# A graph attention layer with a routed feed-forward: where normed input, bias and beta are added for the tiles ahead of the blocks, and the step of the first block

## What is computed

```python
# _layernorm(x): (x - mean) / sqrt(var + 1e-5);  msgs: attention sums of each node, 4 heads of 64
out = msgs.reshape(N, H * D) @ Wo + bo
h = out + _layernorm(x)
gnn = (h - mu) / jnp.sqrt(var + 1e-05) * gamma + beta
x1 = x + gnn
xt = _layernorm(x1)
logits = xt @ Wr + br                      # 8 experts, the top two, weights from a softmax
# the expert network norms once more, then for each of its two experts e:
y_e = gelu(xe @ W1[e] + b1[e]) @ W2[e] + b2[e]      # 256 -> 1024 -> 256
result = x1 + sum(weight_e * y_e)
```

## Time and profile before

| | us |
|---|---|
| median of 3 runs | 3803.58 |
| the runs | 3799.91 to 3803.76 |
| the profiled execution | 3804.72 |
| its span, first to last instruction | 3802.4 |

### The profile page before, as it was taken

One profiled execution on the slowest core, in us unless ns is written; L12 is line 12 of the kernel. 1 busy time (PEld: TensorE's weight loads), 2 busy tenths in 40 slices (PEclk: granted clock), 3 DMA queues, 4 the chain that ended last, 5 costly groups with the idle time before them and its releaser, 6 DMA issues. The chain is left out here.

```text
span 3802.4 us, 76627 instructions
## 1 busy us (share of the span) xinstructions
PE 3098.0 (81%) x21156; PEld 2146.9 (56%) x21156; DVE 1690.1 (44%) x6041; ACT 1507.6 (40%) x4739; POOL 1962.7 (52%) x2036
## 2 busy tenths in 40 slices
PE   8777787778777777877777777787667998899898
PEld 6444444444444444444444444444347898888798
DVE  6154444444444444444444444444475554553222
ACT  5333333333333333333333333333336565564232
POOL 6345555555555555655555555555345444432222
PEclk9888888888888888888888888888758999999999
DMA  6556766676666666666667666666475666665664
GB/s 221 164 150 187 191 190 184 186 191 189 185 185 191 189 185 188 187 192 185 189 187 190 188 185 187 190 188 185 138 230 151 203 203 184 194 180 156 194 181 131
DMA packets 292073, 700.68 MB, mean 184 GB/s; under 512 B 44040, under 2 KB 139679, under 8 KB 291796
## 3 DMA queue, kind: packets, MB, share of 16 engines
q0 software_dynamic: 151888, 455.79, 43.4%
q1 hardware_dynamic: 140036, 243.15, 21.0%
HBM read 632.80 MB, written 65.96 MB: 184 GB/s over the span
## 5 line engine op out<-in xcount | busy, mean ns | idle before, releaser
L246 POOL DMA_INDIRECT e_kv<-d_kv,e_idx x1566 | 1496.1, 955 | 1132.3 <-PE psA L496 668.5
L496 PE MATMUL psA<-e_kv,e_probT 128*32 128x128 f32 x6264 | 529.2, 286 | 297.9 <-issue 292.3
L393 DVE TENSOR_REDUCE e_small<-psD 128x1 f32<-128x384 f32 x261 | 145.5, 558 | 1219.6 <-remote 1208.6
L461 PE MATMUL psK<-consts,e_kv 128*128 128x128 f32 x3132 | 606.6, 327 | 3.3 <-ACT QT L266 1.0
L302 ACT ACTIVATE e_carried<-psA,e_small 128x130 f32<-128x130 f32 x261 | 96.7, 370 | 1135.1 <-PE psA L496 1115.4
L496 PEld LDWEIGHTS psA<-e_kv,e_probT 128*32 128x32 f32 x6264 | 199.9, 108 | 532.8 <-issue 503.8
L461 PEld LDWEIGHTS psK<-consts,e_kv 128*128 128x128 f32 x3132 | 427.5, 166 | 116.4 <-issue 110.0
L1975 PE MATMUL f_psY<-f_w,f_hT 128*128 x1680 | 396.6, 390 | 38.2 <-ACT f_hT L1570 22.1
L1500 POOL DMA_INDIRECT out<-f_y,f_whose x105 | 166.8, 1589 | 479.0 <-DMA out<-f_y,f_whose 281.7
L1962 PE MATMUL f_psH<-f_xT,f_w 128*128 128x128 f32 x3360 | 404.3, 280 | 0.4 <-issue 0.4
L1570 ACT ACTIVATE f_hT<-f_psH,f_b 128x128 f32<-128x128 f32 x840 | 237.6, 372 | 411.0 <-PE f_psH L1962 333.1
(11 more groups left out here) (281 smaller groups left out, 4330.2 us busy)
## 6 DMA issues: line engine op xcount, KB each, us to landing
f_w<-in_W SPq DMA_DIRECT2D x113, 1024.0 KB
e_rows<-d_feat SPq DMA_DIRECT2D x174, 288.0 KB
e_kv<-d_kv,e_idx POOLq DMA_INDIRECT x1566
d_accs<-e_accs SPq DMA_DIRECT2D x87, 195.0 KB
f_xs<-d_xs SPq DMA_DIRECT2D x105, 129.0 KB
d_kv<-p_kv SPq DMA_DIRECT2D x48, 256.0 KB, 2.1
p_x<-in_x SPq DMA_DIRECT2D x49, 128.0 KB, 2.6
n_v<-d_kv SPq DMA_DIRECT2D x49, 128.0 KB
```

Of the source, the lines that this page charges most:

```text
L246: pool.indirect_dma_start(out=kv[g.slot][:, t, :], out_offset=None, in_=kv_dram[:, :], in_offset=bass.IndirectOffsetOnAxis(ap=idx[g.slot][ ...
L461: mm = pe.transpose(psK[:, half, t * P:(t + 1) * P], kv[a.slot][:, third * TS + t, half * P:(half + 1) * P], ident)
L496: mm = pe.matmul(psA[own, 0:2 * HD], probT[c.slot % R][:, j, own], kv[c.slot][:, s * TS + j, D + b * P:D + (b + 1) * P], start=j == 0, sto ...
```

## The change

- For tiles below `PLAIN`, now 13, `project` writes to a bank of `psH` (the tile's parity picks which). Into its upper half go beta, as a product with a row of ones, and x, as a product of x with the identity. Into its lower half go the bias, the normed input (again by the identity) and the projection. All four stand after the wait for ACT's copy.
- DVE's "B" of such a tile is two instructions in place of four: the statistics, straight from the bank. "C" reads both halves of the bank.
- `START` goes from 15 to 14, and with it `PAIRED` and the step of every block: block 0 is in step 14, blocks 7 and 8 in step 21. The steps of the tiles and of the batches stay. The last step is 70. The first blocks of batches 1 to 6 are now in steps 21, 28, 35, 42, 49 and 56, so their fetches stand in the same steps as the last scatters.
- Tiles 13 and 14 get their bias from POOL and go by `psO`.

```diff
-TILE_OPS = dict(A=4, B=4, C=5, D=2, E=1)
+TILE_OPS = dict(A=4, C=5, D=2, E=1)
+ALONE_OPS, BESIDE_OPS = 2, 4
...
-START = RN + 8
+START = RN + 7
...
-    PLAIN = START
+    PLAIN = START - 1
...
-                ready, many = (s_xb, t - PLAIN + 1) if t >= PLAIN else (s_xn, t + 1)
-                return [after(s_po, t + 1, after(ready, many, lambda: dve.tensor_tensor(
+                if t < PLAIN:
+                    return [after(s_po, t + 1, lambda: dve.bn_stats(st[j][:, 0:6], psH[:, t % 2, 0:D])),
+                            (lambda: dve.bn_aggr(st[j][:, 6:8], st[j][:, 0:6]),)]
+                return [after(s_po, t + 1, after(s_xb, t - PLAIN + 1, lambda: dve.tensor_tensor(
                             y[j][:, :], psO[:, 0:D], xn[j][:, :], ALU.add))),
...
+                raw, shifted = (psH[:, t % 2, 0:D], psH[:, t % 2, D:2 * D]) if t < PLAIN else (y[j][:, :], xb[j][:, :])
...
-                    if t >= 1:
-                        pe.wait_ge(s_t["B"], (t - 1) * TILE_OPS["B"] + 1)
+                    if t > PLAIN:
+                        pe.wait_ge(s_t["B"], before("B", t - 1) + 1)
+                    elif 2 <= t < PLAIN:
+                        pe.wait_ge(s_t["C"], before("C", t - 2) + 3)
+                    into = psO if t >= PLAIN else psH[:, t % 2, :]
                     if t < PLAIN:
-                        pe.matmul(psO[:, 0:D], cst("ones")[0:1, :], biaso[0:1, :], start=True, stop=False)
+                        if t == 0:
+                            pe.wait_ge(s_w, 16 * 5)
+                        pe.wait_ge(s_in[t % RL], (t // RL + 1) * 32)
+                        pe.matmul(into[:, D:2 * D], cst("ones")[0:1, :], vec[0:1, 1, :], start=True, stop=False)
+                        pe.matmul(into[:, D:2 * D], ident, x[t % RL][:, :], start=False, stop=True)
+                        pe.wait_ge(s_xn, t + 1)
+                        pe.matmul(into[:, 0:D], cst("ones")[0:1, :], biaso[0:1, :], start=True, stop=False)
+                        pe.matmul(into[:, 0:D], ident, xn[t % RS][:, :], start=False, stop=False)
                     for b in range(DC):
-                        mm = pe.matmul(psO[:, 0:D], turned[s % RS][:, 0, b, :], wo[:, b, :],
+                        mm = pe.matmul(into[:, 0:D], turned[s % RS][:, 0, b, :], wo[:, b, :],
                                        start=t >= PLAIN and b == 0, stop=b == DC - 1)
```

More of the change, by code:

```diff
@@ L1256 @@
 LISTED = max(hi - lo for lo, hi in map(listed_by, range(NK)))
-assert all(step_of(b) >= (batch_of(b) + 1) * RN + 8 for b in range(NB))
+assert all(step_of(b) >= (batch_of(b) + 1) * RN + 7 for b in range(NB))
 def finish(nc, ctx, cst, io, out, dram, rows, ints, spots, wo, lnst, biaso):
@@ L1351, in finish @@
     s_pool = sem("ns_pool")
-    s_t = {k: sem(f"ns_{k}") for k in TILE_OPS}
+    s_t = {k: sem(f"ns_{k}") for k in "ABCDE"}
     s_b = {k: sem(f"ns_{k}") for k in BATCH_OPS}
@@ L1385, in finish @@
     R_AT, S_AT, T_AT = 3, 4, 5
-    PLAIN = START
+    PLAIN = START - 1
+    before = lambda name, t: t * TILE_OPS[name] if name != "B" else (
+        ALONE_OPS * min(t, PLAIN) + BESIDE_OPS * max(t - PLAIN, 0))
     FB = 512 // BK
@@ L1547, in spread @@
             def spread(b):
-                act.wait_ge(s_t["B"], b * TILE_OPS["B"] + 3)
+                act.wait_ge(s_t["B"], before("B", b) + (2 if b < PLAIN else 3))
                 act.activation(st[b % RS][:, 8:9], st[b % RS][:, 7:8], ACT.Sqrt, bias=cst("eps")).then_inc(s_sd[0], 1)
@@ L1588, in _ @@
                     act.wait_ge(s_in[t % RL], (t // RL + 1) * 32)
-                    if t >= RS:
-                        act.wait_ge(s_t["B"], (t - RS) * TILE_OPS["B"] + 1)
+                    if PLAIN <= t - RS:
+                        act.wait_ge(s_t["B"], before("B", t - RS) + 1)
+                    elif t >= RS:
+                        act.wait_ge(s_po, t - RS + 1)
                     act.activation(xn[t % RS][:, :], x[t % RL][:, :], ACT.Identity, bias=lnst[:, t, 1:2],
@@ L1687, in attended @@
                     dve.wait_ge(s_h2, t - RX + 1)
-                return [after(s_sd[0], t + 1, after(s_t["B"], (t + 1) * TILE_OPS["B"],
+                raw, shifted = (psH[:, t % 2, 0:D], psH[:, t % 2, D:2 * D]) if t < PLAIN else (y[j][:, :], xb[j][:, :])
+                return [after(s_sd[0], t + 1, after(s_t["B"], before("B", t + 1),
                                                     lambda: dve.reciprocal(st[j][:, 8:9], st[j][:, 8:9]))),
-                        lambda: dve.scalar_tensor_tensor(out=y[j][:, :], in0=y[j][:, :], scalar=st[j][:, 6:7],
+                        lambda: dve.scalar_tensor_tensor(out=y[j][:, :], in0=raw, scalar=st[j][:, 6:7],
                                                          in1=vec[:, 0, :], op0=ALU.subtract, op1=ALU.mult),
                         lambda: dve.scalar_tensor_tensor(out=x1t, in0=y[j][:, :], scalar=st[j][:, 8:9],
-                                                         in1=xb[j][:, :], op0=ALU.mult, op1=ALU.add),
+                                                         in1=shifted, op0=ALU.mult, op1=ALU.add),
                         (lambda: dve.bn_stats(st[j][:, 0:6], x1t),),
@@ L1839, in started @@
                     if t is not None:
-                        yield from chain(s_t[name], t * TILE_OPS[name], TILE_OPS[name], ops(t))
+                        yield from chain(s_t[name], before(name, t), before(name, t + 1) - before(name, t), ops(t))
                 if s == 0:
@@ L1958, in first_half @@
                 for f in range(FC):
+                    if f == 0 and g == 0:
+                        pe.wait_ge(s_t["C"], before("C", PLAIN - 1) + 3)
                     if f % FB == 0 and g >= 1:
```

## The result

The changed kernel takes 3849.63 us (median of 4 runs, 3846.24 to 3854.01), the kernel before 3801.74 on the same chip (4 runs). The ratio is 1.0123, with a 95% interval of 1.0111 to 1.0135: 47.9 us slower. The forecast was 3861, its range 3832 to 3877. The profiled execution has a span of 3844.4, 42.0 over that of before; the edge pass ends at the same moment in both (PE's first transposition of a tile's messages is at 2745.44 and 2745.40), so all 42 lie in `finish`. What follows accounts for these 42.

A forecast was written before the change was run, and what follows sets the result against it. The prediction took PE's loop, with ACT's copy in series, to bound the steps ahead of the blocks. Its terms 22.5+2.0+13.7+15.2+4 = 57.4 on the profiled 3804.7 gave 3862, median 3861; range 3832 to 3877.

The forecast's parts named there:

- three signs of being wrong: Granted clock of 1.00 before 2860, steps ahead of the blocks under 7 us, or no waits at the batches' first blocks.
- first rival: PE's clock rises ahead of the blocks, steps stay near 5.75 us, some 5 us less up to block 0: 3834; 12%.
- the first term: Block 0's first half comes at 2884.5 against 2862.03, +22.5 us; own range 18 to 28.
- the others: Terms after block 0's start: extra tile step +2.0, batch 1 +13.7, batches 2 to 6 +15.2, clock +4.
- batch 1: At block 7 PE, a step sooner, waits for the rows of the batch's last scatter: +13.7 us, range 9 to 15.
- batches 2 to 6, waits for rows: At these batches' first blocks PE waits 2.8 for batch 2, 3.9 for batch 6, 2.6 to 3.3 between: +15.2 together.
- extra tile step and clock: Tile 14's work beside block 0, +2.0; six new gaps, some of which lower PE's clock, +4, ends 0 and 9.
- a step goes from 5.75 to 8.90: Ahead of the blocks, three more products per tile add 3.15 us behind the wait for ACT's copy, at 1.2 GHz.
- The bounds for the identity products: In each project ahead of the blocks, an identity product costs 0.93 to 1.15 us; 1.00 taken.
- The batches don't bind: Rival: scatters land sooner or PE comes later, so the boundaries' +28.9 and the clock's 4 go: 3828; 8%.
- The hold without a name: Rival: an unexplained hold like DVE's 7.85 falls between block 0's rows and first half, adding 5 to 10: 3869; 5%.
- Faster: Rival: clock rises, steps ahead of the blocks go to 4.9 us, no boundary binds: 3795; 3%.

The follow-up runs named there:

- e3: Changed kernel with PE's wait for ACT's copy moved behind the four added products, so only the projection waits; ratio 1.0059 to the kernel before.
- e7: Kernel before with one difference: PE's existing bias product stands ahead of the wait for ACT's copy; ratio 0.9983, 6.5 us faster than the kernel before.
- e2: Kernel before with START 14 alone: every block one step sooner, no products added; ratio 1.0068, 26 us over the kernel before.
- e9: Changed kernel with products ahead of ACT's copy and every block from 7 on one step later; ratio 1.0020, 7.6 us over the kernel before.
- e1: Changed kernel with START back at 15, the added products staying on PE; ratio 1.0036, 13.8 us over the kernel before.
- e5: Changed kernel with START 15 and PE's wait for ACT's copy behind the four added products; ratio 1.0001 to the kernel before.
- e4: Changed kernel with the turning at the first block of batches 1 to 6 moved behind the second half of the block before, counting and tile's turnings; ratio 1.0095.
- e11: Changed kernel with products ahead of ACT's copy and a batch's seven tiles scattered in two steps, not three; ratio 1.0028, 10.8 us over the kernel before.
- e10: Kernel before with the bias product ahead of ACT's copy, plus two useless identity pairs for each tile below 15; ratio 0.9991 to the kernel before.
- e8: Changed kernel with the four added products reordered to x, beta, bias, normed input; starts sum to 4.17 in place of 4.46; timed once, time not compared.

## Why the prediction was right, and where it wasn't

It was right in sign and range, and in the cause of the larger part. Two of its own three signs of being wrong came all the same: the granted clock was 1.00 well before 2860, and the seven steps up to project 9 took 6.9 us on average, under 7. The third, no waits at the boundaries, didn't. Its forecast was 57.4 on the profiled time and 42.0 came, and the median, 3849.6, lies about midway between the forecast (3861) and its first rival (3834). That it lies in the range is luck in part: the first term had 18 to 28 and came out at 8.2, and the others, though two of them weren't in the sum, made 33.8 where 34.9 was forecast. Of the forecast's own range the upper end should be 3876 by the ends that it names, not 3877. By its own terms:

| term | forecast | measured |
|---|---|---|
| block 0's first half | +22.5 | +8.2 |
| blocks 0 to 6 | 0 | -5.6 |
| batch 1 (first halves of blocks 6 to 9) | +13.7 | +14.7 (wait 13.75) |
| batches 2 to 6, waits for rows | +15.2 | +11.9 |
| their waits for the gelu and others | 0 | +6.0 |
| extra tile step and clock (PE's busy time, blocks 9 to 90) | +2.0 and +4 | +6.6 |

**The products ahead of the blocks: mis-sized by 14.3.** The price of the products was right: at 1.2 GHz a project went from 3.01 to 6.17, +3.15 as summed. The failed step is "a step goes from 5.75 to 8.90", which took the clock of the earlier trace rows as given. It rose in part, so seven steps took 48.2 and not 62.3. The first rival, which the prediction gave 12%, was therefore half of what happened. The argument against it was that the idle 0.93 in each step stays. The pause did stay, 0.73, and the clock rose and fell all the same; e3, which takes it away, went to 0.92. But e7 takes it away too, with 24 us of unbroken work at 0.50, so neither the pause nor the length of a stretch settles the level, and what does stays open. The Trainium skill (TensorE: Matmul & The Clock Gate, "What's actually happening") says that activity releases the throttle, and by that the rival. The traces agree in the kernel after (0.71) and in e3 (0.92), but not in e7, if activity is taken to be the profile's busy time. The prediction had held against it that stretches of 3 us had never raised the clock. That is the length of the products alone: with logits and turnings PE's unbroken stretch before was 4.8 us.

The bounds for the identity products were right too. The rows show 1.15 behind beta, x and bias and 1.01 behind the normed input. The same page ("Step-by-step: what each phase is for") has weight loads pulled ahead where nothing conflicts, by which each would be 0.93; the trace doesn't show that here.

**Block 0.** POOL's train kept its length (24.4 from 2837.80 to 2862.19, before 23.9), and rows to first half took 2.72 in place of 4.75 (forecast 2). Both steps held. "Block 0 is a step earlier by its number and later by the clock" held.

**Blocks 0 to 6** weren't in the sum. They took 71.0 in place of 76.7. From the first half of block 0 to that of block 6 PE's waits for the tiles' normed rows are, in the kernel before and then in the kernel after:

```profile
PE n_psM L1909 <- ACT n_h L1597: 8.2, 4, 3.2
PE n_psM L1909 <- issue: 4.1, 1, 4.1
```

```profile
PE n_psM L1917 <- issue: 5.6, 2, 4.1
PE n_psM L1917 <- ACT n_h L1602: 2.8, 2, 2.3
```

That is 3.9 of the 5.6, and 1.4 is PE's busy time. It comes with START 14 and not with a later block 0: e2, e3 and e9, whose block 0 was earlier than before, took 71.3 to 72.7 here, and e1, whose block 0 was the latest of all, 76.8. Why isn't shown; the sum had set block 0's start and then moved everything by it.

**The boundaries** came out as worked out: 13.75 against 13.7 at block 7, and the scatter-to-turning delay was 4.6 to 5.6 against the 5.65 taken. What the sum left out are the waits ahead of the second half and the small ones, about 1 us in each of five. The step before each boundary grew by them; in step 27 the gelu that PE waited for stood behind 4.70 us in which ACT was idle. e2 shows the whole of the boundaries without the products (13.98 and 11.97), e1 their absence with them, e9 their absence with an early block 0.

**Rivals.** "The batches don't bind" is excluded by e2 and e9. The hold without a name didn't come between block 0's rows and its first half: PE waited 1.21 there. It did come in e1, on the path to block 0. "Faster" is excluded for this change; what it rested on, a rising clock, did come, and e5 shows that without the boundaries it is worth at most a few us.

What stays open: why, with START 14, moving the turning (e4) or the scatters (e11) takes away waits for rows and leaves the stretch from block 9 to 90 as long as it was. The windows show that in the kernel after step 27 is the longer one, with 3.6 us more of POOL's work in it; ACT and DVE stand idle there, unnamed, until POOL's indirect DMAs are over. A kernel that breaks up these trains would be the test, and wasn't made.

## What to carry to other kernels

A step number is a place in an order, not a time: before a consumer is moved a step ahead, measure from the end of the producer's last transfer to the consumer's first use, at every place where the pattern repeats and not at the first alone, because the same shift was paid six times here. Work that is added behind a wait should first be looked at for whether it needs what is waited for: put ahead of it, the same four products cost 12 to 14 us less by the stage and 22 to 25 by the time, and one old product put there gave the only measurable gain of these runs. A granted clock read from the kernel before holds only as long as the engine's work stays the same. And a wait is followed to its end: the engine that a row names may itself be standing.

## What wasn't expected of the hardware

- PE's clock moved between its two levels within a step: once up after 6.6 us without a pause, and down behind a pause of 0.73. With the pause filled by the four products it was 0.88 to 0.92 (e3, e5); with useless products (e10) it was 0.71; and with the one old product (e7) it stayed at 0.50 through 24 us without a pause.
- More work on PE went with quicker steps: steps 2 to 9 took 34.5 in e5, with three product pairs more in each step, against 39.3 in e7; the first two steps, 4.9 slower in e5, made up for it. It isn't steady: the same code took 36.5 in e9 and 39.1 in e11.
- ACT and DVE stood idle for 4 to 13 us, with nothing that the trace names, until a run of indirect DMAs on POOL was over (e1, e11, the kernel after).
- The order of the same four float32 products changed their total at 1.2 GHz from 4.46 to 4.17 (e8).
- The same kernel took 50 us more on some chips than on others, and 35 to 45 of it lay ahead of `finish`.
